# Two layers of attention and feed-forward on one core: the second stage's pieces on TensorE and the quantised tokens' transposes, moved behind both lots of projections

## The chip, the core and the metric

The kernel runs on one core of one Trainium2 chip. The metric is the device time of one execution, in microseconds (us); the kernel before takes 953.4 us, the median of three runs (951.37 to 954.11). The engines that matter are TensorE (PE in the rows; its weight loads are PEld), VectorE (DVE), ScalarE (ACT) and GpSimd (POOL). Each works through its own queue in order, and they wait for each other by semaphores.

## The reference, cut to what matters

`x` is 64 sequences of 128 tokens of width 128, `ctx` 64 contexts of 77 rows.

```
x = x + L0_xattn(ctx, layernorm(x))    # queries from x; keys and values from ctx and x; 8 heads of 64,
                                       # q and k divided by their norms, softmax, Wo, layer norm
x = x + L0_ffn(layernorm(x))           # per token: scale = max|x| / 127, round to int8, times int8 weights
x = x + L1_xattn(layernorm(x), ctx)    # scores = (x We) ctx^T, softmax over the tokens, times ctx, times W2^T
x = x + L1_ffn(layernorm(x))           # router picks one of 8 experts per token: relu(x W1 + b1) W2 + b2
```

## The kernel before, in words

The attention of the first layer is done one sequence at a time, in rounds numbered j; one round of TensorE lasts 10 to 13 us. The quantised matmul and the second attention with its router (the second stage) are done for groups of four sequences, one group every four rounds, with the work of a group spread over the rounds by rho = (j - 2) mod 4. From round 64 on the experts' tiles are interleaved and then stand alone. The order of each engine's work is written out by hand.

In a round j of the middle, TensorE issues in this order:

1. transposes of the normalised q and k of sequence j (L1643), 8 or 12 of them;
2. `slot_a`, a piece of the second stage: L1487 (rho 0), L1496 (rho 1), L1502 (rho 2), L1508 (rho 3);
3. the value projection of sequence j: `product`, three matmuls of 512 columns (L1450, L1451, L1452), once or twice;
4. `slot_b`: for rho 0 the transpose of the router's logits (L1516); for rho 1 the context times W2 (L1526); for rho 2 three transposes of the context (L1533); for rho 3 the context times We (L1539). It writes PSUM bank 7, and waits for that bank by `seven_free`, which is VectorE's `o_cent` (the centring of the attention output, L1309);
5. the query and key projections of sequence j + 1: two or three products. Behind the first of them, for rho 2, `quantised`: four transposes of the quantised tokens (L1583) into PSUM bank 3;
6. `slot_c`: for rho 3 the transposes of the centred tokens (L1573), for rho 0 the counting of the experts (L1552 to L1557) and L1565;
7. attention times values (L1670): the heads 4 to 7, which write bank 4, then `three_emptied`, a wait until bank 3 has been read, then the heads 0 to 3, which write bank 3;
8. the scores of the first 128 keys (L1717), then `seven_emptied`, a wait until bank 7 has been read, the transposes of the tokens of sequence j + 2 (L1743), the transposes of the attention output (L1749, after VectorE's `o_n`, L1357), the scores of the context keys (L1717 or L1722), and Wo (L1765).

Whether a product is done twice in step 3 and three times in step 5 depends on `fresh`: the context rows are packed at 80 rows a sequence into blocks of 128, so five of eight sequences bring a new block. The pattern of `rho` and `fresh` together repeats every eight rounds.

ScalarE follows in a round: copies of q and k (L576, L581), of the values (L598), for rho 1 the second attention's exponentials (L604), the squares of the new q and k (L617, one per product), of which the first is followed for rho 2 by the copy of the quantised tokens (`quantised_copied`, L611), then for rho 1 `v_s` (L634), for rho 2 `ctx_t` (L641), for rho 3 `ke_t` (L646) and `tc_t` (L672), then a logarithm and an exponential (L655, L658) on the way to the inverse norms `rstd`, which GpSimd finishes (L863 to L870), then the big exponentials (L677).

VectorE: statistics of the last round's attention output and `o_cent` (L1289 to L1309), the second stage (`window`), the sums of squares (L1267), `var_in` (L1273), `rden` and `o_n` (L1355, L1357), the scaling of q and k by `rstd` (L1374).

In the rounds 0 to 4 there is no second stage yet; instead four transposes of an expert's W1 (line 1463) stand in `slot_b` and four of its W2 in `slot_c`, copied by ScalarE after the squares (L626, L568); `three_emptied` waits for the second copy.

Of the kernel before, what the change touches and what calls it, by code (L numbers as in the profile page):

```python
# [58 lines left out]
def whole(nc, x_res, ctx_res, ident, w1_all, w2_all, table, sent, padded, sorted_rows, out, x, ctx, mask,  # L59
# [16 lines left out]
    with ExitStack() as stack:  # L76
# [256 lines left out]
        def fresh(pos):  # L333
            return pos % LAP in FRESH
# [50 lines left out]
        def has(b, inside):  # L385
            return inside or 0 <= b < B

        def group(g, inside):
            return inside or 0 <= g < NG
# [11 lines left out]
        def after(eng, name, g, inside):  # L401

            if inside or g >= 0:
                eng.wait_ge(s[name], g + 1)
# [10 lines left out]
        def tail(j, inside):  # L415
            return not inside and j >= TAIL
# [107 lines left out]
        def _(act):  # L524
# [45 lines left out]
            def run(j, par, rho, g, inside, pos, turn):  # L570
# [36 lines left out]
                def quantised_copied():  # L607
                    if rho == 2 and group(g, inside):

                        after(act, "qT_done", g, inside)  # L610
                        nc.scalar.activation(qq_t[:, :, :], g_qt, ACT.Copy).then_inc(s["qt_copied"], 1)  # L611

                if has(j + 1, inside):

                    for n in range(3) if fresh(pos + 1) else range(2):
                        act.wait_ge(qk_done, 3 * j + 4 + n)
                        nc.scalar.activation(sq[:, n * INNER:(n + 1) * INNER], ps_qk[:, n, :],  # L617
                                             ACT.Square).then_inc(sq_done, 1 if n == 0 or fresh(pos + 1) else 2)
                        if n == 0:
                            quantised_copied()  # L620
                if tail(j, inside):
                    tile(tile_no(j, 0))
                if not inside and 0 <= j < E - AHEAD:
# [97 lines left out]

            act.wait_ge(setup_g, FIRST_G)
            run(-3, 1, 3, -3, False, -3, 0)
            masks(FIRST_MASKS, None)
            act.wait_ge(ld_ln, 4 * 16)
            run(-2, 0, 0, -2, False, -2, 0)
            act.dma_start(wo_sb[:, :, :], Wo.rearrange("(t p) d -> p t d", p=P)).then_inc(ld_late, 16)

            rounds_written_out(run)
            at, turns = NA, (T - 1 - NA) // 4  # L730
            for k in range(REST[0], at):
# [715 lines left out]
        def _(pe):  # L1447
            def product(dst, tok_hi, tok_lo, w):

                nc.tensor.matmul(dst, tok_hi, w_hi[:, w:w + INNER], start=True, stop=False)  # L1450
                nc.tensor.matmul(dst, tok_hi, w_lo[:, w:w + INNER], start=False, stop=False)  # L1451
                return nc.tensor.matmul(dst, tok_lo, w_hi[:, w:w + INNER], start=False, stop=True)  # L1452

            def seven_free(j, inside):

                if has(j - 2, inside):
                    pe.wait_ge(o_cent, j - 1)
                elif has(j + 1, inside):
                    pe.wait_ge(xct_sb, j + 2)

            def flip(bank, raw):
                for c in range(C):
                    last = nc.tensor.transpose(ps[:, bank, c * P:(c + 1) * P], raw[:, c * P:(c + 1) * P], ident[:, :])
                return last
# [46 lines left out]
            def slot_b(j, rho, g, inside):  # L1511

                if rho == 0 and group(g - 2, inside):

                    after(pe, "lt_copied", g - 2, inside)
                    nc.tensor.transpose(ps[:, 3, P:2 * P], lg_t[:, :], ident[:, :]).then_inc(s["lg_done"], 1)  # L1516
                if not inside and 0 <= j < E - AHEAD:

                    seven_free(j, inside)
                    pe.wait_ge(ld_exp[j + AHEAD], 32)  # L1520
                    flip(7, w1_all[:, j + AHEAD, 0:F]).then_inc(s["wT_done"], 1)
                if rho == 1 and group(g - 1, inside):

                    seven_free(j, inside)
                    for i in range(G):
                        last = nc.tensor.matmul(g_seven[0:M, i, :], ctx_t[:, i, :], w2_t[:, :], start=True, stop=True)  # L1526
                    last.then_inc(s["v2_done"], 1)
                if rho == 2 and group(g, inside):

                    seven_free(j, inside)  # L1530
                    after(pe, "ctx_taken", g, inside)
                    for i in range(3):
                        last = nc.tensor.transpose(g_seven[:, i, :], ctx_now[:, i, :], ident[:, :])  # L1533
                    last.then_inc(s["ctxT_done"], 1)
                if rho == 3 and group(g, inside):

                    seven_free(j, inside)
                    after(pe, "ctx_copied", g, inside)
                    nc.tensor.matmul(ps[:, 7, 0:G * M], we_t[:, :], ctx_t[:, :, :].rearrange("p g m -> p (g m)"),  # L1539
                                     start=True, stop=True).then_inc(s["ke_done"], 1)  # L1540
# [35 lines left out]
            def quantised(j, rho, g, inside):  # L1576

                if rho == 2 and group(g, inside):

                    after(pe, "q2_done", g, inside)  # L1580
                    after(pe, "x3_done", g - 1, inside)
                    for i in range(G):
                        last = nc.tensor.transpose(g_qt[:, i, :], q_bf[:, i, :], ident_bf[:, :])  # L1583
                    last.then_inc(s["qT_done"], 1)
# [52 lines left out]
            def run(j, par, rho, g, inside, pos, turn):  # L1637
# [11 lines left out]
                if has(j, inside):  # L1649
# [3 lines left out]
                    for kt in (0, 1) if fresh(pos) else (0,):  # L1653
# [1 line left out]
                            pe.wait_ge(setup_v, SETUP_V)  # L1655
                        last = product(ps_v[kt], xc_hi[:, par, kt, :], xc_lo[:, par, kt, :], 2 * INNER)
                        last.then_inc(v_done, 1 if fresh(pos) else 2)
                slot_b(j, rho, g, inside)
                if not inside and j == TOTAL_AT:
                    after(pe, "before_done", g - 2, inside)  # L1660
                    count(4)
# [12 lines left out]
                if has(j + 1, inside):  # L1674

                    pe.wait_ge(lo_done, j + 2)
                    for n, (src, w) in enumerate(((0, 0), (0, INNER), (1, INNER)) if fresh(pos + 1) else ((0, 0), (0, INNER))):

                        if has(j, inside):
                            if n == 0:  # L1680
                                pe.wait_ge(q_copied, j + 1)
                            else:
                                pe.wait_ge(k_copied, 2 * j + n)
                        last = product(ps_qk[:, n, :], xc_hi[:, 1 - par, src, :], xc_lo[:, 1 - par, src, :], w)
                        last.then_inc(qk_done, 1 if n == 0 or fresh(pos + 1) else 2)
                        if n == 0:
                            quantised(j, rho, g, inside)
                else:
                    quantised(j, rho, g, inside)
                slot_c(j, rho, g, inside)  # L1690
                if has(j - 1, inside):

# [80 lines left out]

            pe.wait_ge(setup_g, FIRST_G)
            run(-3, 1, 3, -3, False, -3, 0)
            keep_busy(32)
            run(-2, 0, 0, -2, False, -2, 0)
            keep_busy(16)
            pe.wait_ge(setup_g, SETUP_G)
            pe.wait_ge(setup_v, 3)  # L1780

            def run_and_setup(j, par, rho, g, inside, pos, turn):
                run(j, par, rho, g, inside, pos, turn)
                if not inside and j == -1:

                    first_weights((4, 5))
                    pe.wait_ge(s["w_taken"], 1)
                    pe.wait_ge(setup_v, 4)
                    nc.tensor.transpose(ps[:, 5, 0:P], mask_f[:, :], ident[:, :]).then_inc(s_maskT, 1)
# [76 lines left out]
```

## Time and profile before

| what | value |
|---|---|
| time, median of 3 runs | 953.4 us (951.37 to 954.11) |
| profiled execution, span | 950.6 us |
| PE busy | 912.8 us, 96% |
| DVE busy | 744.9 us, 78% |
| ACT busy | 693.5 us, 73% |
| POOL busy | 458.1 us, 48% |
| granted clock of TensorE, mean | 0.997 |

The profiled execution is given by its span; the median of the timed runs is 2.8 us above it. Matmuls are pipelined: the record of a 512-column matmul lasts 0.40 us, but the next one starts 0.23 us after it. What a matmul costs is therefore read from start to start, and a wait on TensorE from how much later than usual the next start comes.

### The profile page before, as it was taken

How to read it: one execution, taken by the hardware profiler on the slowest of the kernel's cores; microseconds unless marked ns; L12 is line 12 of the kernel's file. 1: busy time of each engine (PE TensorE's matmuls, PEld its weight loads, DVE VectorE, ACT ScalarE, POOL GpSimd, SP SyncE). 2: the span in 40 equal slices, each digit the busy share in tenths (PEclk: the TensorE clock that was granted, in tenths of full speed). 3: DMA queues.
4: the chain of work that ended last, by engine and by line, in shares of the span. 5: the costliest groups of instructions: out<-in, count | busy, mean ns of one | idle time of the engine just before them, and what ended most of it. 6: DMA issues, size and time to landing. Idle time of an engine off the chain costs nothing.

```text
span 950.6 us, 30821 instructions
## 1 busy us (share of the span) xinstructions
PE 912.8 (96%) x11286; PEld 794.5 (84%) x11286; DVE 744.9 (78%) x2526; ACT 693.5 (73%) x1671; POOL 458.1 (48%) x1094
## 2 busy tenths in 40 slices
PE   7999999999999999999999999999999999899997
PEld 6788888788878887888788878888888878898997
DVE  5566787888888888888888888888888978877553
ACT  4877777677778787778777777777778766676664
POOL 5422433354535453545354444444454545777554
PEclk9999999999999999999999999999999999999999
DMA  7743000000000000000000000000000022245310
GB/s 196 200 124 57 2 2 2 2 13 2 14 2 14 2 14 2 13 3 10 5 10 5 8 8 8 7 8 7 8 8 8 7 47 71 61 97 106 95 55 20
DMA packets 45193, 31.44 MB, mean 33 GB/s; under 512 B 11555, under 2 KB 40166, under 8 KB 45046
## 3 DMA queue, kind: packets, MB, share of 16 engines
q1 hardware_dynamic: 39398, 19.93, 9.2%
q0 software_dynamic: 4320, 8.50, 2.8%
q8 instruction: 92, 1.51, 0.7%
q10 hardware_dynamic: 1328, 1.06, 0.4%
q14 instruction: 55, 0.45, 0.2%
HBM read 17.75 MB, written 12.17 MB: 31 GB/s over the span
## 4 chain that ended last, share of the span: by engine, by line
PE 69%; DVE 14%; ACT 8%; issue 3%; POOL 3%; DMA 1%; SPq 1%; DVEq 0%; POOLq 0%; ACTq 0%
PE ps L1670 9%; PE ps L1717 9%; PE ps L1643 7%; PE ps L1765 6%; PE ps L1450 5%; PE ps L1622 5%; PE ps L1630 5%; PE ps L1452 5%; PE ps L1451 5%; DVE sumsq L1267 4%; PE ps L1722 3%; ACT probs L604 2%; PE ps L1749 2%; ACT qk_hat L617 2%; PE ps L1496 1%
## 5 line engine op out<-in xcount | busy, mean ns | idle before, releaser
L1374 DVE TENSOR_TENSOR qk_hat<-ps,rstd 128x512 f32<-128x512 f32 x168 | 106.3, 684 | 49.2 <-POOL rstd L870 49.1
L1267 DVE TENSOR_REDUCE sumsq<-qk_hat 128x8 f32<-128x512 f32 x168 | 107.8, 677 | 35.9 <-ACT qk_hat L617 34.7
L863 POOL TENSOR_TENSOR rs_t<-rs_y 128x32 f32<-128x32 f32 x73 | 17.9, 245 | 235.2 <-ACT rs_y L658 235.2
L1670 PE MATMUL ps<-v_x,prob 128*64 128x65 f32 x2048 | 127.9, 225 | 2.1 <-ACT w_all L568 0.4
L1670 PE MATMUL ps<-v_c,prob 128*64 128x65 f32 x2048 | 124.2, 222 | 0.0
L677 ACT ACTIVATE prob<-ps,neg_shift 128x512 f32<-128x512 f32 x128 | 88.4, 690 | 48.6 <-PE ps L1717 48.6
L1670 PEld LDWEIGHTS ps<-v_x,prob 128*64 128x64 f32 x2048 | 105.0, 137 | 20.9 <-issue 19.2
L617 ACT ACTIVATE qk_hat<-ps 128x512 f32<-128x512 f32 x168 | 98.5, 599 | 31.7 <-PE ps L1452 25.8
L1450 PE MATMUL ps<-w_hi,xc_hi 128*128 128x512 f32 x272 | 120.8, 444 | 0.8 <-POOL xc_lo L835 0.8
L1717 PE MATMUL ps<-qT_all,kT_all 64*128 64x128 f32 x1536 | 111.6, 285 | 2.3 <-ACT prob L677 1.1
L1452 PE MATMUL ps<-w_hi,xc_lo 128*128 128x512 f32 x272 | 107.3, 395 | 0.0
L1451 PE MATMUL ps<-w_lo,xc_hi 128*128 128x512 f32 x272 | 106.6, 392 | 0.0
L1670 PEld LDWEIGHTS ps<-v_c,prob 128*64 128x64 f32 x2048 | 105.1, 138 | 0.0
L1717 PEld LDWEIGHTS ps<-qT_all,kT_all 64*128 64x128 f32 x1536 | 93.2, 187 | 13.6 <-ACT prob L677 8.9
L782 POOL DMA_INDIRECT out_dram<-prob,x_res x71 | 71.9, 1013 | 43.0 <-DVE prob L943 28.5
L1643 PE MATMUL ps<-ident,qk_hat 128*128 128x128 f32 x672 | 85.4, 275 | 0.5 <-DVE qk_hat L1374 0.5
L677 ACT ACTIVATE prob<-ps,mask_now 128x512 f32<-128x512 f32 x128 | 82.3, 708 | 0.3 <-PE ps L1722 0.2
L792 POOL DMA_INDIRECT sorted_rows<-stage,idx x64 | 70.5, 1102 | 16.0 <-issue 14.9
L1643 PEld LDWEIGHTS ps<-ident,qk_hat 128*128 128x128 f32 x672 | 76.7, 143 | 1.0 <-DVE qk_hat L1374 1.0
L1765 PE MATMUL ps<-wo_sb,o_t 128*128 128x128 f32 x512 | 74.1, 288 | 0.9 <-ACT o_t L698 0.7
L1630 PE MATMUL ps<-w_all,kT_all 128*128 x568 | 74.7, 275 | 0.0
L1765 PEld LDWEIGHTS ps<-wo_sb,o_t 128*128 128x128 f32 x512 | 61.9, 191 | 12.3 <-ACT o_t L698 8.0
(245 smaller groups left out, 2257.2 us busy)
## 6 DMA issues: line engine op xcount, KB each, us to landing
x_res<-sorted_rows SPq DMA_DIRECT2D x71, 65.5 KB, 1.9
w_all<-in_L_ffn_W_dram SPq DMA_DIRECT2D x16, 256.0 KB, 5.3
sorted_rows<-fill SPq DMA_DIRECT2D x8, 327.5 KB
out_dram<-prob,x_res POOLq DMA_INDIRECT x71
sorted_rows<-stage,idx POOLq DMA_INDIRECT x64, 2.4
ctx_res<-in_ctx_dram SPq DMA_DIRECT2D x8, 115.5 KB
x_res<-in_x_dram SPq DMA_DIRECT2D x1, 768.0 KB
sorted_rows<-fill SPq DMA_DIRECT2D x1, 524.0 KB, 5.0
```

Of the source, the lines that this page charges most:

```text
L617: nc.scalar.activation(sq[:, n * INNER:(n + 1) * INNER], ps_qk[:, n, :], ACT.Square).then_inc(sq_done, 1 if n == 0 or fresh(pos + 1) else 2)
L677: nc.scalar.activation(prob[:, n // 2, n % 2 * INNER:(n % 2 + 1) * INNER], ps_s[n], ACT.Exp, bias=(mask_now[:, par:par + 1] if n > 1 else ...
L1267: nc.vector.reduce_sum(sumsq[:, n * H:(n + 1) * H], sq[:, n * INNER:(n + 1) * INNER].rearrange("p (h d) -> p h d", d=DH), AX).then_inc(ss_ ...
L1374: nc.vector.tensor_tensor(qk_hat[:, n * INNER:(n + 1) * INNER].rearrange("p (h d) -> p h d", d=DH), ps_qk[:, n, :].rearrange("p (h d) -> p ...
L1450: nc.tensor.matmul(dst, tok_hi, w_hi[:, w:w + INNER], start=True, stop=False)
L1451: nc.tensor.matmul(dst, tok_hi, w_lo[:, w:w + INNER], start=False, stop=False)
L1452: return nc.tensor.matmul(dst, tok_lo, w_hi[:, w:w + INNER], start=False, stop=True)
L1630: last = nc.tensor.matmul(ps_y[k % 2], h_t[(k - 2) % 4][:, c, :], flat(w2_all[:, bass.ds(e, 1), c * P:(c + 1) * P]), start=c == 0, stop=c ...
L1643: last = nc.tensor.transpose(ps_qk[:, n, t * P:(t + 1) * P], qk_hat[:, n * INNER + t * P:n * INNER + (t + 1) * P], ident[:, :])
L1670: last = nc.tensor.matmul(dst[half:half + DH, :], prob[:, kt, col + half:col + half + DH], v, start=kt == 0, stop=kt == 1)
L1717: last = nc.tensor.matmul(ps_s[2 * kt + half][:, cols], keys, q_t[rows, cols], start=True, stop=True)
L1765: last = nc.tensor.matmul(ps_o, o_t[:, t * P:(t + 1) * P], wo_sb[:, t, :], start=t == 0, stop=t == PAIRS - 1)
```

## The change

On TensorE, `slot_b` stays between the value projection and the query and key projections only for rho 0 (and in the last rounds, in which no sequence follows); for rho 1, 2 and 3 it now stands behind all query and key projections. `quantised` moves from behind the first query projection to behind the last key projection, ahead of `slot_b`. On ScalarE the copy of the quantised tokens moves from behind the first square to behind the last. No instruction is added or taken away.

```diff
@@ ScalarE
                         nc.scalar.activation(sq[:, n * INNER:(n + 1) * INNER], ps_qk[:, n, :],
                                              ACT.Square).then_inc(sq_done, 1 if n == 0 or fresh(pos + 1) else 2)
-                        if n == 0:
-                            quantised_copied()
+                    quantised_copied()
@@ TensorE
-                slot_b(j, rho, g, inside)
+                between = rho == 0 or not has(j + 1, inside)
+                if between:
+                    slot_b(j, rho, g, inside)
@@ TensorE
                         last.then_inc(qk_done, 1 if n == 0 or fresh(pos + 1) else 2)
-                        if n == 0:
-                            quantised(j, rho, g, inside)
-                else:
-                    quantised(j, rho, g, inside)
+                quantised(j, rho, g, inside)
+                if not between:
+                    slot_b(j, rho, g, inside)
                 slot_c(j, rho, g, inside)
```

TensorE, a round with rho 3 in the middle, before. L1508 is `slot_a`, L1539 `slot_b`, L1573 `slot_c`; the three lines L1450 to L1452 are one product.

```order
L1508 MATMUL ps<-wq_t,qq_t 128x128 x4
L1450 MATMUL ps<-w_hi,xc_hi 128x512
L1451 MATMUL ps<-w_lo,xc_hi 128x512
L1452 MATMUL ps<-w_hi,xc_lo 128x512
L1539 MATMUL ps<-ctx_t,we_t 128x308
L1450 MATMUL ps<-w_hi,xc_hi 128x512
L1451 MATMUL ps<-w_lo,xc_hi 128x512
L1452 MATMUL ps<-w_hi,xc_lo 128x512
```

The same place of the changed kernel (its lines are numbered one lower here: L1538 is `slot_b`, L1572 `slot_c`); the first rows are the last two products.

```order
L1449 MATMUL ps<-w_hi,xc_hi 128x512
L1450 MATMUL ps<-w_lo,xc_hi 128x512
L1451 MATMUL ps<-w_hi,xc_lo 128x512
L1449 MATMUL ps<-w_hi,xc_hi 128x512
L1450 MATMUL ps<-w_lo,xc_hi 128x512
L1451 MATMUL ps<-w_hi,xc_lo 128x512
L1538 MATMUL ps<-ctx_t,we_t 128x308
L1572 MATMUL ps<-ident,t_c 128x128 x4
```

The context times We has moved from behind the value projection to directly ahead of the transposes of `slot_c`.

ScalarE, a round with rho 2, before. L617 are the squares, L611 the copy of the quantised tokens, L641 that of the context.

```order
L598 ACTIVATE v_x<-ps 128x8x64
L598 ACTIVATE v_c<-ps 128x8x64
L617 ACTIVATE qk_hat<-ps 128x512
L611 ACTIVATE qq_t<-ps 128x512
L617 ACTIVATE qk_hat<-ps 128x512
L641 ACTIVATE ctx_t<-ps 128x308
```

The same place of the changed kernel.

```order
L598 ACTIVATE v_x<-ps 128x8x64
L598 ACTIVATE v_c<-ps 128x8x64
L617 ACTIVATE qk_hat<-ps 128x512 x2
L611 ACTIVATE qq_t<-ps 128x512
L640 ACTIVATE ctx_t<-ps 128x308
```

The squares stand together, and the copy of the quantised tokens behind them.

## Rows read from the trace of the kernel before

**Rows 1.** The page, busy time of each engine.

```profile
PE 912.8 (96%) x11286; PEld 794.5 (84%) x11286; DVE 744.9 (78%) x2526; ACT 693.5 (73%) x1671; POOL 458.1 (48%) x1094
```

**Rows 2.** Waits of TensorE: us in total, times, longest.

```profile
PE ps L1539 <- DVE o_c L1309: 3.6, 7, 0.6
PE ps L1749 <- DVE o_n L1357: 3.0, 13, 0.5
```

**Rows 3.** Timeline of TensorE, rho 3, round from 457.05: start, us, instruction, [idle before].

```profile
458.67 0.40 PE L1452 MATMUL ps<-w_hi,xc_lo 128*128 128x512 f32 x1
459.63 0.79 PE L1539 MATMUL ps<-ctx_t,we_t 128*128 128x308 f32 x2 [0.57 <-DVE o_c L1309]
...
462.10 0.39 PE L1452 MATMUL ps<-w_hi,xc_lo 128*128 128x512 f32 x1
462.33 0.60 PE L1573 MATMUL ps<-ident,t_c 128*128 128x128 f32 x4
462.86 0.34 PE L1670 MATMUL ps<-v_x,prob 128*64 128x65 f32 x4
...
463.72 0.29 PE L1670 MATMUL ps<-v_c,prob 128*64 128x65 f32 x4
464.07 0.34 PE L1670 MATMUL ps<-v_x,prob 128*64 128x65 f32 x4
...
466.42 0.60 PE L1749 MATMUL ps<-ident,o_n 128*128 128x128 f32 x4
```

**Rows 4.** Timeline of ScalarE in the same round.

```profile
461.15 1.97 ACT L617 ACTIVATE qk_hat<-ps 128x512 f32<-128x512 f32 x3 [1.39 <-PE ps L1452]
...
463.33 0.60 ACT L672 ACTIVATE tc_t<-ps 128x512 f32<-128x512 f32 x1
```

**Rows 5.** Timeline of VectorE in the same round.

```profile
459.23 0.35 DVE L1309 SCALAR_TENSOR_TENSOR o_c<-ps,o_stat,lno_w 128x128 f32<-128x128 f32 x1
...
465.26 0.21 DVE L1355 RECIPROCAL rden<-ps 128x8 f32<-128x8 f32 x1 [0.29 <-PE ps L1670]
465.51 0.69 DVE L1357 TENSOR_TENSOR o_n<-ps,rden 128x512 f32<-128x512 f32 x1
```

**Rows 6.** Timeline of ScalarE, rho 2, round from 396.76.

```profile
401.59 0.60 ACT L617 ACTIVATE qk_hat<-ps 128x512 f32<-128x512 f32 x1 [0.43 <-PE ps L1452]
402.09 0.59 ACT L611 ACTIVATE qq_t<-ps 128x512 bf16<-128x512 bf16 x1
402.59 1.29 ACT L617 ACTIVATE qk_hat<-ps 128x512 f32<-128x512 f32 x2
...
404.90 0.23 ACT L655 ACTIVATE rs_ln<-var_in 128x32 f32<-128x32 f32 x1 [0.71 <-DVE var_in L1273]
```

**Rows 7.** Timeline of TensorE in that rho 2 round.

```profile
400.36 0.49 PE L1533 MATMUL ps<-ident,ctx_now 128*128 128x128 f32 x3
...
401.40 0.40 PE L1583 MATMUL ps<-ident_bf,q_bf 128*128 128x128 bf16 x4
...
402.84 0.40 PE L1452 MATMUL ps<-w_hi,xc_lo 128*128 128x512 f32 x1
403.17 0.34 PE L1670 MATMUL ps<-v_x,prob 128*64 128x65 f32 x4
```

**Rows 8.** Timeline of TensorE, rho 3, round from 409.20, at the wait for bank 3.

```profile
415.49 0.29 PE L1670 MATMUL ps<-v_c,prob 128*64 128x65 f32 x4
415.90 0.34 PE L1670 MATMUL ps<-v_x,prob 128*64 128x65 f32 x4
```

**Rows 9.** Timeline of TensorE, round 3 (an early one), at the wait for bank 3.

```profile
61.72 0.29 PE L1670 MATMUL ps<-v_c,prob 128*64 128x65 f32 x4
62.15 0.34 PE L1670 MATMUL ps<-v_x,prob 128*64 128x65 f32 x4
```

**Rows 10.** Timeline of ScalarE, rho 1, round from 432.29.

```profile
440.81 1.13 ACT L634 ACTIVATE v_s<-ps,sinv 77x128 f32<-77x128 f32 x4 [1.20 <-DVE sinv L1185]
```

**Rows 11.** Timeline of VectorE, rho 0, round from 469.18.

```profile
472.74 0.19 DVE L1071 TENSOR_TENSOR lg<-ps,br_b 128x32 f32<-128x32 f32 x1 [1.00 <-PE ps L1516]
```

## The prediction

> **What bounds the kernel now.** I read the busy times first. TensorE is busy for 912.8 of 950.6 us and nobody else is above 78% [rows 1], and in the middle the chip grants it nearly full clock (mean 0.997, in the table). So the length is TensorE's own stream plus its waits, and a change that only reorders can win only waits. The list of its waits comes next: the largest is that of L1539, the context times We, for `o_cent` of VectorE, 3.6 us in 7 times [rows 2]. The timeline of one such round shows the true price: the value projection's last matmul starts at 458.67, its successor is due 0.23 us later (as at 462.10 and 462.33) and comes at 459.63, so the round loses 0.73, of which the profile shows 0.57 as idle and 0.16 lies under the modelled end of the matmul before [rows 3]. The same round has a second stop that the list of waits doesn't show: between the fourth and the fifth head of L1670 the start comes 0.35 after the last one, where 0.12 is the pace, so 0.23 is lost [rows 3]. It ends 0.14 after ScalarE's `tc_t` (463.33 + 0.60 = 463.93) [rows 4], which is what `three_emptied` waits for. The other kind of rho 3 round loses 0.41 - 0.12 = 0.29 there [rows 8]. The rounds repeat every eight, so these two stand for all.
>
> **The change part by part.** Nothing is added or removed: each moved piece costs what it cost. A product takes 0.69 from start to start (three times 0.23).
>
> *Rho 3.* L1539 goes behind the two or three products. In the round shown the query projection then starts at 458.90 instead of L1539, the three products end at 460.97, and L1539 comes due when `o_cent` (459.23 + 0.35 = 459.58 [rows 5]) is 1.4 us old. The wait is gone. Over the run that is 3.6 us of idle time and 7 times 0.16, 4.7 us. What was behind it comes 0.73 earlier: L1573 at 461.60, L1670 at 462.13, the fifth head due 0.98 later, at 463.11. Is bank 3 empty by then? A square starts 0.19 after the start of what follows its product (L1583 at 401.40, the square at 401.59 [rows 6, 7]), so the last one starts at 461.16 and ends near 461.8. `ke_t` follows, and `tc_t` can start when L1573 is through, 0.6 plus 0.1 after its start, at 462.3, ends at 462.9 and releases TensorE at 463.04. That is 0.07 before it is needed, so this 0.23 goes too, 7 times, 1.6 us. In the six rounds of the other kind L1573 keeps its time; the squares are ready 0.5 sooner, `tc_t` goes from being last in its queue to waiting for L1573 alone, and the 0.29 goes for the same reason, 1.7 us. Of what is late next: `tc_t`, by less than 0.1.
>
> *Rho 2, 14 rounds.* In the round shown the query product starts at 400.36 in L1533's place. The squares then start at 401.24, 401.93 and 402.62 instead of 401.59, 402.59 and after it [rows 6, 7]. L1583 stands from 402.43, L1533 behind it, and L1670 comes where it is, at 403.17. The copy L611 now follows the last square: 403.2 to 403.8, TensorE may write bank 3 at 403.94, and needs it at 403.17 + 0.98 = 404.15. There are 0.2 us to spare, so no stall; it is hidden by the heads 4 to 7. If that cover were gone, each 0.1 would cost 1.4 us over the run. The logarithm L655, which waits 0.71 for `var_in` at 404.90 [rows 6], comes some 0.6 sooner, and with it `rstd` and the next round's VectorE work. That wins nothing by itself, since TensorE doesn't wait for it there, but it is the lead that VectorE needs in rho 3.
>
> *What the order itself costs TensorE.* No row shows three f32 transposes directly behind bf16 ones. The nearest are L1573, four transposes ahead of L1670, 0.53, and a product ahead of L1670, 0.33 instead of 0.23 [rows 3, 7]: entering L1670 costs 0.10 in both, and a transpose 0.11. Bounds are therefore 0.10 less and 0.10 more per moved piece of rho 2, plus or minus 2.8 us over 28 pieces. I take nothing for it, and 0.7 us of loss for the thin margins together (26 of `tc_t` and `qq_t` at about 0.03).
>
> *Rho 1, 13 rounds.* L1526 goes behind, its reader `v_s` waits 1.20 for VectorE's `sinv` and starts at 440.81 [rows 10], while L1526 would start at 437.9 (the round's start 432.29, 12 and 8 transposes at 0.11, five products at 0.69) and be through about 1.0 later. The squares there stand behind ScalarE's own exponentials (L604), which the change leaves alone. Nothing is won; the waits of L1749 [rows 2] stay, since the chain that ends in them starts at the value projection.
>
> *Rho 0* is not touched; VectorE waits 1.00 there for TensorE [rows 11], so it moves along.
>
> *Rounds 1, 3 and 4.* The W1 transposes move behind the products too; the squares and the two copies behind them start 0.35 sooner, and the stop at bank 3, 0.43 - 0.12 = 0.31 [rows 9] and 0.37 in the two shorter ones, goes: 1.0 us.
>
> The sum: 4.7 + 1.6 + 1.7 + 1.0 = 9.0 (9.1 unrounded), less 0.7, is 8.4 us. The profiled execution would go from 950.6 to 942.2. The median lies 2.8 above it, and I keep that: **945.0 us**.
>
> **Rivals.** *A, VectorE takes the wait over in rho 3.* TensorE would reach L1749 at 466.42 - 0.96 = 465.46, but `o_n` ends at 466.20. `rden` waits 0.29 for TensorE [rows 5], so without a lead VectorE could bring it forward by that alone, to 465.91; half of the 0.96 stays lost, 0.5 in 7 rounds, and the time is 948.6. For it: that 0.29 is much less than the 0.96. Against it: the 0.6 that the earlier squares of rho 2 give.
>
> *B, the copy of the quantised tokens comes too late; this one can end slower.* The place is `three_emptied` in rho 2. If ScalarE is one square (0.6) later than I put it, 0.4 is exposed in 14 rounds, 5.6 us: 950.6. If two, 1.0 is, 14 us: 945.0 + 14 = 959.0, slower than before. It decides from about 1.1 us of lateness: then the 0.86 exposed eats the whole 9 us and 3 more. For it: L611 leaves an empty place (0.43 of waiting ahead of the first square [rows 6]) for the busiest one. Against: the squares come 0.35 sooner, and the margin is positive in my sum.
> The Trainium skill ("Perfetto Trace Analysis", section "Optimizing Tensor Performance") says that independent groups of matmuls should rotate through the PSUM banks, so that the reading out of one lies beside the matmuls of the next. The change goes against it: bank 3 is filled by L1583 some 1.7 us ahead of its next writer instead of 2.7. By the rule this is rival B; by the rows the heads 4 to 7, in another bank, are just cover enough.
>
> *C, nothing is won:* the time given back at L1539 comes back at L1749 or another of the waits in rho 1, because the round is a loop through all engines, not TensorE's stream: 953.4. Against it: ScalarE or VectorE waits for TensorE in every round shown [rows 4, 5, 6, 11] but that of rho 1 [rows 10].
>
> *D, the projections in one piece are cheaper,* the lower bound above: 942.2.
>
> **Chances.** The forecast 0.66, A 0.14, B 0.06 (half of it slower), C 0.09, D 0.05. A measurement of this kernel tells apart about 0.3%, 2.9 us. Below 950.5 lie the forecast, A and D, with a little of B: 0.86. Within: C and the mild half of B, 0.10. Slower: 0.04, B and what I haven't seen. The range that leaves out less than 2 in 10 goes from D with its margins kept, 941.0, to A and mild B, 951.0. The forecast alone would be 942.5 to 947.5.
>
> **What would show it.** In the profile after: L1539's line without a wait for o_c; the rho 3 round that ran from 457.05 to 469.18 shorter by 0.96 and the other kind by 0.29, no gap over 0.12 inside L1670; in rho 2 none either (a gap there is B); in rho 3 L1749 without an idle time before it (one is A); rho 0 and rho 1 as long as before; the squares of rho 2 with no 0.43 before the first. I would be wrong if the rounds of rho 3 kept their length, or if `tc_t` or L611 released a late fifth head.

## The result and the profile after

| | before | changed |
|---|---|---|
| time, median | 952.38 us (951.36 to 954.11, 4 runs) | 939.75 us (939.26 to 940.51, 4 runs) |
| ratio | | 0.9865, 95% interval 0.9851 to 0.9879 |
| span of the profiled execution | 950.6 us | 938.4 us |
| PE busy | 912.8 us | 905.8 us |
| granted clock, mean | 0.997 | 0.996 |

The change made the kernel 1.35% faster, in the direction that was forecast, but by more: 939.75 lies below the range's low end of 941.0. The line numbers of the changed kernel differ from those of before by one here and there (L1449 to L1451 are a product; L1538, L1572 and L1671 are the L1539, L1573 and L1670 of before; L1356 writes `o_n`, L1308 writes `o_c`).

TensorE's waits after, in the columns of [rows 2]:

```profile
PE ps L1749 <- DVE o_n L1356: 3.8, 15, 0.5
...
PE ps L1551 <- DVE onehot L1089: 2.9, 7, 0.4
```

The wait of the context times We for `o_cent`, 3.6 us in [rows 2], is in the list no more. The wait of L1749 has grown from 3.0 to 3.8: it comes in 15 rounds now, and most of what is new is 0.55 in round 61, the last with rho 3.

The same long rho 3 round as in [rows 3], timeline of TensorE (start, us, instruction); it now runs from 449.80 to 461.01, 11.21 us instead of 12.13:

```profile
451.43 0.40 PE L1451 MATMUL ps<-w_hi,xc_lo 128*128 128x512 f32 x1
451.66 0.39 PE L1449 MATMUL ps<-w_hi,xc_hi 128*128 128x512 f32 x1
...
453.73 0.68 PE L1538 MATMUL ps<-ctx_t,we_t 128*128 128x308 f32 x2
454.25 0.60 PE L1572 MATMUL ps<-ident,t_c 128*128 128x128 f32 x4
...
455.65 0.29 PE L1671 MATMUL ps<-v_c,prob 128*64 128x65 f32 x4
455.76 0.29 PE L1671 MATMUL ps<-v_x,prob 128*64 128x65 f32 x4
...
456.80 1.16 PE L1717 MATMUL ps<-qT_all,kT_all 64*128 64x128 f32 x16
```

The query product starts 0.23 after the value product's last matmul, with no hole, and between the fourth and fifth head (455.65 to 455.76) there is only the pace of 0.12. Both stops of [rows 3] are gone. ScalarE in that round, for [rows 4]:

```profile
452.55 1.98 ACT L617 ACTIVATE qk_hat<-ps 128x512 f32<-128x512 f32 x3
454.45 0.43 ACT L645 ACTIVATE ke_t<-ps 128x308 f32<-128x308 f32 x1
454.89 0.60 ACT L671 ACTIVATE tc_t<-ps 128x512 f32<-128x512 f32 x1
457.40 0.23 ACT L654 ACTIVATE rs_ln<-var_in 128x32 f32<-128x32 f32 x1 [1.91 <-DVE var_in L1272]
```

`tc_t` ends at 455.49, 0.27 before the fifth head starts; less the 0.14 that the release takes, a margin of 0.13 where the prediction had 0.07. And VectorE, for [rows 5]:

```profile
449.00 1.55 DVE L1402 COPY v_c<-v_c 64x512 f32<-64x512 f32 x2
450.57 0.30 DVE L1288 BATCH_NORM_STATS2 o<-ps 128x6 f32<-128x128 f32 x1
...
451.70 0.35 DVE L1308 SCALAR_TENSOR_TENSOR o_c<-ps,o_stat,lno_w 128x128 f32<-128x128 f32 x1
...
457.29 0.17 DVE L1198 COPY x_res<-rstd 128x4 f32<-128x4 f32 x1
457.36 0.20 DVE L1354 RECIPROCAL rden<-ps 128x8 f32<-128x8 f32 x1
457.59 0.69 DVE L1356 TENSOR_TENSOR o_n<-ps,rden 128x512 f32<-128x512 f32 x1
```

`rden` has no idle time before it, where [rows 5] had 0.29 for TensorE: VectorE is now the one that is late. TensorE's tokens are transposed (L1743) at 457.89 and L1749 should follow 0.17 later, at 458.06; `o_n` ends at 458.28 and L1749 starts at 458.34. This is rival A, in a size of 0.28; some 0.1 of it comes back behind L1749, where the scores follow after 0.59 instead of 0.67. The profile's list of idle times doesn't carry it, since the modelled end of L1743 (458.22) covers most of it.

A rho 2 round after, for [rows 6] and [rows 7], TensorE and then ScalarE. It is one of the kind with two query and key products, where [rows 6] and [rows 7] show one with three:

```profile
442.79 0.39 PE L1451 MATMUL ps<-w_hi,xc_lo 128*128 128x512 f32 x1
443.01 0.40 PE L1582 MATMUL ps<-ident_bf,q_bf 128*128 128x128 bf16 x4
443.25 0.50 PE L1532 MATMUL ps<-ident,ctx_now 128*128 128x128 f32 x3
443.68 0.34 PE L1671 MATMUL ps<-v_x,prob 128*64 128x65 f32 x4
...
444.54 0.29 PE L1671 MATMUL ps<-v_c,prob 128*64 128x65 f32 x4
444.66 0.29 PE L1671 MATMUL ps<-v_x,prob 128*64 128x65 f32 x4
```

```profile
442.53 1.34 ACT L617 ACTIVATE qk_hat<-ps 128x512 f32<-128x512 f32 x2
443.76 0.59 ACT L611 ACTIVATE qq_t<-ps 128x512 bf16<-128x512 bf16 x1
```

The copy of the quantised tokens ends at 444.35 and the fifth head starts on time at 444.66, so rival B didn't come. The first square has no wait before it.

**Where the 12.2 us of the span came from.** From the start of L1643 in one round to the next, summed over the rounds of a kind (us, after less before):

| rounds | forecast | measured |
|---|---|---|
| rho 3, from round 5 on | -8.0 | -8.16 (long ones -0.92 four times and -1.11 twice, the others -0.33 to -0.37, round 61 -0.11) |
| rho 2, from round 8 on | +0.7 with the margins of rho 3 | -1.41 (-0.06 to -0.14 each) |
| rho 0 | 0 | -0.60 (-0.26 in round 10, -0.05 to -0.07 in every second other) |
| rho 1 | 0 | -0.03 |
| rounds 1, 3, 4 | -1.0 | -1.29 |
| up to the end of round 0 | 0 | -0.44 |
| from the start of round 63 on | 0 | -0.27 |

Rounds are called long and short within their rho: before, 12.1 and 11.9 us for rho 3 (the long ones have the wait for `o_c`), 12.2 and 11.2 for rho 0, 12.9 and 11.9 for rho 1.

### The profile page after: what moved, and what is told of

The parts are those of the page before. It is cut to its first block, busy times and chain, and to the rows that moved or that the text cites. A ratio compares the mean times of both kernels' runs of the same rounds, so it can differ in the third digit from the quotient of the medians.

```text
span 938.4 us, 30821 instructions
## 1 busy us (share of the span) xinstructions
PE 905.8 (97%) x11286; PEld 796.8 (85%) x11286; DVE 744.7 (79%) x2526; ACT 694.8 (74%) x1671; POOL 459.0 (49%) x1094
## 4 chain that ended last, share of the span: by engine, by line
PE 65%; DVE 21%; ACT 6%; issue 4%; POOL 2%; DMA 1%; SPq 1%; DVEq 1%; POOLq 0%; ACTq 0%
PE ps L1717 8%; PE ps L1671 8%; PE ps L1642 7%; PE ps L1765 6%; PE ps L1621 5%; PE ps L1629 5%; DVE sumsq L1266 5%; PE ps L1449 4%; PE ps L1451 4%; PE ps L1450 4%; PE ps L1722 2%; PE ps L1749 2%; ACT probs L604 2%; PE ps L1495 1%; DVE qk_hat L1373 1%
## 5 line engine op out<-in xcount | busy, mean ns | idle before, releaser
L1671 PE MATMUL ps<-v_x,prob 128*64 128x65 f32 x2048 | 126.2, 225 | 0.3 <-ACT probs L604 0.2
L1671 PE MATMUL ps<-v_c,prob 128*64 128x65 f32 x2048 | 123.0, 222 | 0.0
L1449 PE MATMUL ps<-w_hi,xc_hi 128*128 128x512 f32 x272 | 113.6, 418 | 0.8 <-POOL xc_lo L834 0.8
L1671 PEld LDWEIGHTS ps<-v_x,prob 128*64 128x64 f32 x2048 | 103.6, 138 | 12.0 <-issue 11.3
L1717 PE MATMUL ps<-qT_all,kT_all 64*128 64x128 f32 x1536 | 111.6, 285 | 1.5 <-ACT prob L676 0.6
L617 ACT ACTIVATE qk_hat<-ps 128x512 f32<-128x512 f32 x168 | 97.2, 599 | 13.6 <-PE ps L1451 3.8
L1451 PE MATMUL ps<-w_hi,xc_lo 128*128 128x512 f32 x272 | 106.8, 393 | 0.0
L1450 PE MATMUL ps<-w_lo,xc_hi 128*128 128x512 f32 x272 | 106.5, 391 | 0.0
L1717 PEld LDWEIGHTS ps<-qT_all,kT_all 64*128 64x128 f32 x1536 | 93.2, 187 | 12.4 <-ACT prob L676 6.9
L1671 PEld LDWEIGHTS ps<-v_c,prob 128*64 128x64 f32 x2048 | 103.6, 138 | 0.0
```

The costliest lines, as they stand in the source:

```text
L1671: last = nc.tensor.matmul(dst[half:half + DH, :], prob[:, kt, col + half:col + half + DH], v, start=kt == 0, stop=kt == 1)
L1717: last = nc.tensor.matmul(ps_s[2 * kt + half][:, cols], keys, q_t[rows, cols], start=True, stop=True)
```

## The experiments

Two theories on the large term, rho 3. Theory P (place): the wait for `o_c` goes because L1539 stands later, the wait for bank 3 because the squares are earlier; both within the round. Theory L (lead): the earlier squares of rho 2 give VectorE a lead through the sums, the logarithm and `rstd`, and that lead alone would have taken the wait for `o_c`, and is needed to use the rest. Shares in us by kind of round are read as above. All kernels of this section are variants of the changed one.

**e1_rho3: only rho 3 moved.**

```diff
-                between = rho == 0 or not has(j + 1, inside)
+                between = rho != 3 or not has(j + 1, inside)
```
and `quantised` and its copy back behind the first query projection and the first square.

> Only the pieces of rho 3 (L1539 and, in round 1, the W1 transposes) stand behind the projections; rho 1, rho 2 and the quantised tokens as before. Theory P (place: the wait for o_c goes because L1539 comes after it, the wait for bank 3 because the squares are early, both within the rho 3 round): the rho 3 rounds win what they won in the full change, 5.9 us in the six long ones, 2.1 in the six others, 0.5 in round 1, about 8.6 us, ratio to before 0.9910. Theory L (lead: the rho 3 round can only use it because the earlier squares of rho 2 put VectorE 0.6 us ahead): L1749 then waits for o_n by up to 0.5 more in the long rounds, and about 3 to 3.6 us less is won, ratio 0.9945.

Measured 946.66 us, ratio 0.9935 (0.9918 to 0.9953). The interval holds theory L's 0.9945 and leaves out theory P's 0.9910. The rho 3 rounds win 6.14 instead of 8.16: 0.64 to 0.66 in the long ones, and 0.33 to 0.38 in the others, as in the full change. TensorE's waits:

```profile
PE ps L1753 <- DVE o_n L1357: 5.8, 21, 0.5
```

L1753 is the L1749 of before here. It waits 21 times, where it waited 13 times in [rows 2]. Six of the new ones are in the long rounds, 0.38 to 0.40 each. VectorE in one of them, from the sums to `o_n`:

```profile
460.76 1.27 DVE L1267 TENSOR_REDUCE sumsq<-qk_hat 128x8 f32<-128x512 f32 x2
462.06 0.18 DVE L1273 TENSOR_SCALAR var_in<-sumsq 128x24 f32<-128x24 f32 x1
...
462.29 0.20 DVE L1355 RECIPROCAL rden<-ps 128x8 f32<-128x8 f32 x1
462.53 0.69 DVE L1357 TENSOR_TENSOR o_n<-ps,rden 128x512 f32<-128x512 f32 x1
```

`rden` follows without a pause, so VectorE sets the pace. The round starts at 454.48, so `rden` stands 7.81 into it, against 7.56 in the full change. The short rho 0 rounds also lose 0.04 to 0.09 each, the lateness being handed on to `onehot`. TensorE reaches the place of L1749 1.12 sooner than before and starts it only 0.58 sooner: this is rival A as the prediction worked it out, about half of the gain lost, when there is no lead. Place alone wins two thirds of the long rounds' gain; the rest needs the lead.

**e2_not_rho3: the change without its rho 3 part.**

```diff
-                between = rho == 0 or not has(j + 1, inside)
+                between = rho in (0, 3) or not has(j + 1, inside)
```

> The change without its rho 3 part: L1539 stays between the value and the query projection. Theory P: only the order of rho 2 (1.4 us over 14 rounds), rho 0 (0.6) and the early rounds 0, 3 and 4 (about 1.4) are left, 3.4 us, ratio to before 0.9964; the idle time ahead of L1539 stays at 0.57. Theory L: o_c comes 0.6 us sooner in the rho 3 rounds since VectorE has its lead from rho 2, so the idle time ahead of L1539 shrinks to near zero by itself, another 4 us are won and the ratio is 0.992; only the wait for bank 3 stays.

Measured 946.15 us, ratio 0.9927 (0.9912 to 0.9942): theory L's 0.992 lies in the interval, theory P's 0.9964 does not. The wait that the move was to remove is nearly gone with the context times We (L1538 here) left in its place:

```profile
PE ps L1538 <- DVE o_c L1308: 0.8, 3, 0.3
```

0.8 us instead of 3.6. The long rho 3 rounds win 0.61 to 0.65 four times and 0.28 twice, the other kind nothing, since its wait for bank 3 stays. Rho 2 wins 1.29 and rounds 3 and 4 0.82, nearly as in the full change; rho 0 wins 0.27 of the 0.60, since round 10 keeps its length here. The two parts overlap: 0.66 and 0.6 in a long round make 0.92 to 1.11 together, not 1.3, since both remove the same wait.

**e3_quant: only the quantised tokens and their copy.**

```diff
-                between = rho == 0 or not has(j + 1, inside)
+                between = True
```

> Only the quantised tokens' transposes and their copy are moved; all of slot_b stays where it was. Theory P: at most 0.07 us a round from the bf16 transposes no longer standing ahead of a product, 1.0 us if they are cheap ahead of L1670 too, ratio to before 0.999; the wait for o_c stays 0.57. Theory L: the second square comes 0.2 to 0.5 us earlier and gives VectorE a lead of that size, so the wait for o_c falls to 0.1 to 0.4 and 2 to 3 us more are won, ratio 0.996.

Measured 952.21 us, ratio 0.9988 (0.9978 to 0.9999). The time is theory P's (0.999) and not theory L's (0.996), but the waits are theory L's: that for `o_c` falls to about half,

```profile
PE ps L1538 <- DVE o_c L1308: 1.9, 7, 0.3
```

and the long rho 3 rounds win 0.27 to 0.30, but the rho 2 rounds lose up to 0.09 each, 0.66 in all. Where they lose it, TensorE at the quantised tokens and at the fifth head:

```profile
451.11 0.40 PE L1582 MATMUL ps<-ident_bf,q_bf 128*128 128x128 bf16 x4
451.44 0.34 PE L1671 MATMUL ps<-v_x,prob 128*64 128x65 f32 x4
...
452.31 0.29 PE L1671 MATMUL ps<-v_c,prob 128*64 128x65 f32 x4
452.50 0.34 PE L1671 MATMUL ps<-v_x,prob 128*64 128x65 f32 x4
```

0.19 from the fourth to the fifth head instead of 0.12, and ScalarE's copy of the quantised tokens ends at 452.45, 0.05 before the fifth head starts:

```profile
451.86 0.59 ACT L611 ACTIVATE qq_t<-ps 128x512 bf16<-128x512 bf16 x1
```

This is rival B in small. From the first head to L1717 TensorE takes 2.15 there (451.44 to 453.59), where it took 2.02 before and 2.01 in the changed kernel, so the stop costs 0.13. That the copy holds the head is read from the code, where `three_emptied` waits for nothing else in these rounds; in rho 3 the head followed its copy by 0.14, not 0.05, and why is open. With the context transposes between the quantised tokens and the heads, as in the full change, there is 0.33 more cover and the stop is not there.

**e8_ctx_only: only the context transposes of rho 2.**

```diff
-                between = rho == 0 or not has(j + 1, inside)
+                between = rho != 2 or j < E - AHEAD or not has(j + 1, inside)
```
and the quantised tokens as before.

> Of the change only the context transposes of rho 2 (L1533) behind the projections; the quantised tokens, rho 1, rho 3 and the early rounds as before. The part without rho 3 had shortened the long rho 3 rounds by about 0.62 and the quantised tokens alone by 0.29. Theory L (the lead is handed on through squares, sums and rstd): this edit alone starts the first square of rho 2 0.35 earlier and shortens the long rho 3 rounds by 0.3 to 0.6, some 2 to 3.6 us, ratio to before 0.997; the order of the pieces gives 0 to 0.08 a round of rho 2 more. Rival S (only both squares together make a lead, as ScalarE's copy of the quantised tokens still stands between them): rho 3 stays within 0.1 of before, ratio 1.000.

Measured 951.04 us, ratio 0.9975 (0.9963 to 0.9987). The long rho 3 rounds win 0.24 to 0.28 and the wait is down again:

```profile
PE ps L1539 <- DVE o_c L1309: 2.0, 7, 0.3
```

Each half of the rho 2 part gives about 0.28 a long round, both together about 0.6 in four rounds and again 0.28 in two; the next experiment's traces say why. The rounds win a little less than the 0.3 at theory L's low end, while its ratio of 0.997 lies in the interval; the rival, with 1.000, does not.

**e4_stage: the full change, the early rounds as before.**

```diff
-                between = rho == 0 or not has(j + 1, inside)
+                between = rho == 0 or j < E - AHEAD or not has(j + 1, inside)
```

> The full change but for the early rounds, in which the transposes of the experts' W1 stay between the projections. By the account of the traces the rounds 0, 1, 3 and 4 gave 1.9 us of the 12; without them the kernel should be at about 941.6, 1.9 us above the full change, ratio to before 0.9885. A rival, that they only run ahead into waits for the inputs' transfers and give it back, has it at 939.8, ratio 0.9865.

Measured 942.59 us, ratio 0.9891 (0.9875 to 0.9908). The expected 0.9885 lies in the interval and the rival's 0.9865 just below it. The rounds 1, 3 and 4 are as long as before, and give 1.3 in the full change. The 0.44 of the start that I had counted in is not the change's: this kernel, which leaves round 0 alone, ends it 0.54 sooner than before. Over the ten profiles of this study round 0 ends between 30.4 and 34.3 us from the start, with the edit in it or not, and TensorE waited 1.2 to 4.0 us for the experts' weights ahead of it. In this kernel five of the six long rho 3 rounds win 1.10 to 1.15, in the changed one only two do; this is 0.6 us of why its profile is only 0.9 us longer than the changed kernel's (939.3 to 938.4), while the timed medians lie 2.8 apart.

What divides these rounds stands in the traces: two copies on VectorE (L1403 before, L1402 here), ahead of everything that VectorE does in the round. The long round of [rows 3], before, with GpSimd's `xc_lo`:

```profile
457.05 1.01 DVE L1403 COPY v_c<-v_c 64x512 f32<-64x512 f32 x2
456.06 0.73 POOL L835 TENSOR_TENSOR xc_lo<-xc_t,xc_hi 128x256 fp32r<-128x256 f32 x1
```

The same round in the changed kernel (its copies were shown above, 449.00 for 1.55), and in this one:

```profile
448.81 0.85 POOL L834 TENSOR_TENSOR xc_lo<-xc_t,xc_hi 128x256 fp32r<-128x256 f32 x1
```

```profile
450.06 1.28 DVE L1402 COPY v_c<-v_c 64x512 f32<-64x512 f32 x2
450.07 0.99 POOL L834 TENSOR_TENSOR xc_lo<-xc_t,xc_hi 128x256 fp32r<-128x256 f32 x1
```

Before, and in e1_rho3, the copies start with the round, behind `xc_lo`, and last 1.01. With the lead they start 0.8 to 0.9 ahead of the round, beside `xc_lo`, and both last longer. Either they start 0.80 ahead, 0.19 behind `xc_lo`, and last about 1.55, or 0.90 ahead, together with it, and last 1.28. So 0.10 of lead more ends `o_c` 0.36 sooner (at 1.89 instead of 2.25 into the round; 2.53 before). All 48 long rho 3 rounds of the eight kernels with a lead are of one kind or the other, and it decides what they win: 0.61 to 0.65 or 0.27 to 0.28 in e2_not_rho3, 0.24 to 0.30 in the two halves of the rho 2 part, where all twelve have the 1.55, and 1.10 to 1.17 or 0.90 to 0.94 with both parts of the change (1.04 to 1.08 for the second in e9_all). That the copies and GpSimd's instructions hold each other up is read from these durations; no run took one of them away. Nor is it known whether a kernel's rounds keep their kind from one execution to the next, as there is one profile of each.

**e5_rho1_dve: the changed kernel, VectorE reordered in rho 1.**

```diff
+                if not tail(j, inside):
+                    sinv_now(j, rho, g, inside)
                 if has(j + 1, inside) and (inside or j != -1):
                     sums_of_squares(j, pos)
...
                                             rden[:, :, :].unsqueeze(3).to_broadcast(four), ALU.mult).then_inc(on_done, 1)
+                if not tail(j, inside):
+                    q_rounded(j, rho, g, inside)
```
The two functions hold what stood in `later` for rho 1.

> The full change, and on VectorE in rho 1 (up to round 63) sinv ahead of the sums of squares and the rounding of the tokens (L1192 of before, four instructions, 0.88 us) behind o_n, where VectorE now waits 1.4 us for rstd. Theory V (the rho 1 rounds are bound by VectorE's o_n): the wait of L1749 in them goes, 0.3 to 0.45 in 13 rounds, 4 to 5 us on top of the change, about 935, ratio to before 0.981. Rival: ScalarE's exponentials, which stand behind v_s, are next, and less than 1.5 us is won, ratio 0.985.

Measured 937.14 us, ratio 0.9834 (0.9818 to 0.9850), 2.6 us below the changed kernel by the medians. The rho 1 rounds win 4.08 (0.60 in round 7, 0.23 in the long ones, 0.30 to 0.34 in the short ones), and L1749's wait for `o_n` (L1757 here) is left in round 61 alone. Its successor is ScalarE's exponential, the scores' wait for bank 6:

```profile
PE ps L1730 <- ACT prob L676: 1.5, 9, 0.2
```

Of the 1.5, 1.2 stands in seven of the long rho 1 rounds, 0.17 each, and was not there in the changed kernel. By the rounds theory V holds at its lower end and the rival takes part of the rest. The time alone doesn't decide: 0.981 lies just outside the interval and 0.985 at its edge. The profile is 2.4 us shorter, not 4.1, as round 0 ends 0.7 later, the rounds 29 and 60 are 0.2 longer each and the part from round 63 on 0.4.

**e6_rank: the changed kernel, the counting of the experts behind the transposes.**

```diff
 def slot_c(j, rho, g, inside):
...
+    if rho == 0 and group(g - 1, inside):     # transposes of t_b, tbT_done
     if rho == 0 and group(g - 2, inside):     # counting, waits for oh_done
-    if rho == 0 and group(g - 1, inside):     # transposes of t_b, tbT_done
```

> The full change, and on TensorE in rho 0 the transposes of the normalised tokens (L1565 of before, 0.44 us) ahead of the counting of the experts (L1552 to L1557), which waits 0.4 for onehot in seven rounds. Theory: the transposes cover the wait, 0.45 in seven rounds, about 3 us on top of the change, ratio to before 0.983. Rival: VectorE's place, which stands ahead of its sums of squares, comes later by the same amount in the other seven rounds and is paid for through rstd: no gain or a loss, ratio 0.987.

Measured 939.46 us, ratio 0.9846 (0.9829 to 0.9864). The long rho 0 rounds win 0.46 to 0.50 as expected and the wait for `onehot` is gone; the short ones lose about 0.1 and the short rho 1 rounds behind the long ones 0.1. From round 6 to round 63 its profile is 2.9 us better than the changed kernel's. The timed ratio lies between the theory's 0.983 and the rival's 0.987, and its interval overlaps the changed one's, so timing alone doesn't tell the two kernels apart; the losses in the short rounds are the rival's, in part.

**e9_all: both, and VectorE's small instructions behind `o_n`.**

```diff
-                if not tail(j, inside):
-                    later(j, par, rho, g, inside)
...
                 if not tail(j, inside):
                     q_rounded(j, rho, g, inside)
+                    later(j, par, rho, g, inside)
```

> The full change with both reorderings of the last two kernels, and on VectorE the small instructions of rho 0 and rho 3 that stand ahead of rden (L1172 to L1181, L1198, L1199 of before) behind o_n as well. If theory V holds, o_n in the long rho 3 rounds comes 0.15 sooner and the rest adds up: 4.5 + 3 + 1 us below the change, about 931, ratio to before 0.978. If the waits only change places, it is at the better of the two, 0.981.

Measured 933.05 us, ratio 0.9788 (0.9771 to 0.9805): faster than both kernels, 6.7 us below the changed one. The expected 0.978 lies in the interval, the 0.981 doesn't. TensorE's longest waits now lie at the start and in the tail; of those above this is left, and one of 0.4 for `o_n` in round 61:

```profile
PE ps L1729 <- ACT prob L676: 1.5, 9, 0.2
```

The short rounds' loss of the last kernel is gone, and the long rho 3 rounds are 1.04 to 1.13 shorter than before. In those with the 1.55 us copies `rden` stands 7.41 into the round instead of 7.55, the 0.15 that was expected of the third edit; what it gives by itself was not tried.

## Why the prediction was wrong

The forecast was 945.0, the time 939.75, 5.25 us lower and outside the range. The step that failed is the term for what the order itself costs TensorE: it was put at nothing, with 0.7 us of loss beside it, and the rho 2 rounds gained 1.41. The rest is in smaller terms and in how the span was turned into a time. Two lines of before are needed for it, the starts of L1717 in the rounds of [rows 3] and [rows 8]:

```profile
465.16 1.16 PE L1717 MATMUL ps<-qT_all,kT_all 64*128 64x128 f32 x16
```

```profile
416.98 1.16 PE L1717 MATMUL ps<-qT_all,kT_all 64*128 64x128 f32 x16
```

The steps one by one:

- *TensorE's stream bounds, only waits can be won.* Right in the main, and too strict: 1.0 us and perhaps 1.4 came from the stream itself, in rho 2.
- *Rho 3, 8.0 us.* Measured 8.16. The two stops are the right ones, but that the sum fits is partly luck, since errors of both signs cancel. The stops were priced too low, as the prediction read each from a single gap. From the value product's last matmul to the transposes of `t_c` a long round took 3.66 (458.67 to 462.33) and takes 2.82 (451.43 to 454.25): the wait for `o_c` cost 0.84, not 0.73. In a short round, which has no such wait, the same work took 1.91 from L1539 to L1573 (412.18 to 414.09) and takes 1.90 now (405.43 to 407.33), so the 0.11 goes with the wait and not with the order. From the fourth head to L1717 a long round took 1.44 (463.72 to 465.16) and takes 1.15, a stop of 0.29 and not 0.23; a short one took 1.49 (415.49 to 416.98) and takes 1.15, 0.34 and not 0.29. So L1717 comes 1.11 sooner in the long round, where the sum had 0.96. Against that, in four of six long rounds 0.2 went to rival A, which was not an alternative but came beside the forecast. And in round 61, where about 0.6 was in the sum, A took nearly all: L1749 waits 0.55 for `o_n` there, and the round is only 0.11 shorter.
- *"That wins nothing by itself"*, said of the lead from rho 2. This step is wrong: without any move of L1539 the lead takes 2.8 of the 3.6 us (e2_not_rho3), and without the lead the move alone keeps a third less in the long rounds (e1_rho3). The prediction needed the lead to refute A, and didn't carry it back to the wait it had just counted. The sum was not hurt, as the two overlap; and rho 0, which "moves along", gives 0.6: 0.05 to 0.07 in every second round, where `onehot` was late by 0.06 and the lead suffices, and 0.26 in round 10, which only the kernels with both parts of the change have.
- *What the order costs, nothing, less 0.7 for the margins.* This is the step that failed: measured a gain of 1.41 in rho 2, an error of 2.1 us. In [rows 7] the quantised transposes and the context transposes cost 0.64 together between the products: 403.17 - 400.36 less three products at 0.69, that is 0.74, less 0.10 at the entry of L1670. After, they cost 0.57 in either kind of round (443.68 - 443.01 - 0.10), and the round shown, of the kind with two products, is 0.09 shorter. The kind of [rows 7] wins 0.09 to 0.14; what lies above 0.07 there was not traced. The four bf16 transposes take 0.24 ahead of f32 transposes (443.01 to 443.25), and 0.29 ahead of a product (in e8_ctx_only from 402.20 to the product's second matmul at 402.72, less its 0.23). That they are cheaper away from a product is measured; why is not. The bound of minus 2.8 held it, but I took the middle, and then subtracted for margins that all held (0.13 and 0.17 us).
- *Rounds 1, 3 and 4, 1.0.* Measured 1.29; the stops at bank 3 were read from one gap here too.
- *Rho 1 nothing.* Right, 0.03.
- *The median lies 2.8 above the span.* For the changed kernel it lies 1.35 above. This one assumption is 1.45 of the 5.25, and has nothing to do with the change. On record every timed run is 1.7 to 1.8 us longer than its own span; the rest of the 2.8 was that the profiled execution of before was one of the short ones. The median of before itself moved from 953.4 to 952.4 with one more run, and was 953.3 in 17.

The errors sum to 2.1 (rho 2) + 0.6 (rho 0) + 0.3 (early) + 0.1 (rho 3) + 0.4 and 0.3 (start and tail) + 1.45 = 5.25. The rivals: A came in part and was paid for within the term; B's wait appears only when the quantised tokens move alone, 0.13 in the round shown; C is refuted by the result; D was the nearest (942.2), for half the right reason. The Trainium skill ("Perfetto Trace Analysis", section "Optimizing Tensor Performance") asks that independent groups of matmuls rotate through the PSUM banks, so that one is read out beside the matmuls of the next. The trace of e3_quant agrees, with its 0.13; that of the changed kernel shows that 0.33 us of other work covers the cost here. The range was too narrow on the side of gain: every term left out of it was a small gain, and the spread of the median over the span was not in it.

## What to carry to other kernels

A wait on a nearly full engine has two ends: what waits can be moved later, or what releases it can be brought forward some rounds up, and a reorder often does both; price them apart, since they don't add. Price a stop from start to start over the whole stretch that it interrupts, not from the one gap or from the idle time of the list. When an engine that was waiting loses its wait, look at once at the instruction that it feeds next: here `o_n` came next, and the next gain lay in moving VectorE's work that nobody was waiting for behind it, into a wait of VectorE's own (4.1 us in the rho 1 rounds; 6.7 us by the medians with TensorE's and VectorE's further reorders). A lead on one engine can also be eaten by the engine beside it: the copies that started 0.8 us sooner took 0.54 longer.

## What the runs showed of the hardware that was not expected

Four bf16 transposes of 128x128 cost 0.29 to 0.30 us ahead of a 512-column product and 0.24 ahead of f32 transposes, and three f32 transposes 0.31 to 0.33 in either place. Two VectorE copies of 64x512 lasted 1.01 us together when they started behind GpSimd's 128x256 subtraction `xc_lo`, 1.28 when they started with it and 1.55 when they started 0.19 behind its start, while `xc_lo` lasted 0.73, 0.99 and 0.85. An idle time of 0.57 on TensorE stood for 0.84 of lost time, 0.73 up to the start that waited and 0.11 behind it, and a wait of 0.28 for none in the list, as the modelled end of the matmul before lies over it.
